# A perceiver layer's first chunk of tokens: order on GpSimd, two banks for its halves, and 48 turns of the identity on TensorE

## What is computed

```python
def reference(x, ctx, w_q, w_kv, w_out, b_out, ...):     # x 32x64x256, ctx 32x1601x192, all float32
    x = x + xattn(layernorm(x), ctx, w_q, w_kv, w_out, b_out)   # 16 heads of 64
    x = x + rwkv(layernorm(x), decay, first, mixes, Wk, Wv, Wr, Wo, bo)
    x = x + relu(layernorm(x) @ w1 + b1) @ w2 + b2
    return x

def xattn(query, context, w_q, w_kv, w_out, b_out):
    q = query @ w_q
    k, v = split(context @ w_kv)
    attn = softmax(q k^T / 8)
    return (attn v) @ w_out + b_out

def layernorm(x):
    return (x - mean(x)) / sqrt(var(x) + 1e-5)
```

## Time and profile before

| | before |
|---|---|
| median of 3 executions | 2353.97 us (2352.03 to 2357.43) |
| the profiled execution, its own time | 2352.82 us |
| its span, first to last instruction | 2351.0 us |
| mean granted TensorE clock | 0.997 |
| busy: PE / DVE / POOL / ACT | 97% / 77% / 70% / 66% |
| start of the first product of `queries(0)` | 18.02 us |
| start of the first product of `with_keys(0)` | 24.58 us |
| start of the first scores of the attention | 134.42 us |

### The profile page before, as it was taken

The page is one execution under the profiler, slowest core; times in us unless marked ns, Lnnn a source line. Parts: engine busy times, 40 slices in busy tenths (PEclk is TensorE's granted clock), DMA queues, the critical chain, the costliest instruction groups (busy, mean ns, idle before and its releaser), DMA issues.

```text
span 2351.0 us, 43942 instructions
## 1 busy us (share of the span) xinstructions
PE 2291.5 (97%) x13696; PEld 2097.1 (89%) x13696; DVE 1812.6 (77%) x3664; ACT 1542.7 (66%) x2696; POOL 1646.7 (70%) x858
## 2 busy tenths in 40 slices
PE   7979999999999999999999999999999999899999
PEld 5769999999999999999999999999999998878788
DVE  7867777777777777777777777777777777679884
ACT  6756666666666666666666666666666666565444
POOL 4238878888888888888888888888888886421111
PEclk9999999999999999999999999999999999999999
DMA  8988888888888888888888888888888886987000
GB/s 228 267 199 189 196 196 197 199 199 200 198 200 199 199 199 199 199 201 199 199 199 199 199 200 199 200 199 200 199 199 199 199 199 162 212 197 198 8 10 28
DMA packets 410273, 438.97 MB, mean 187 GB/s; under 512 B 82528, under 2 KB 380896, under 8 KB 410208
## 3 DMA queue, kind: packets, MB, share of 16 engines
q1 hardware_dynamic: 394384, 427.23, 77.3%
q10 hardware_dynamic: 15824, 10.91, 2.0%
HBM read 167.42 MB, written 52.43 MB: 94 GB/s over the span
## 4 chain that ended last, share of the span: by engine, by line
POOL 44%; issue 25%; PE 18%; SPq 5%; DVE 4%; DMA 2%; ACT 2%; POOLq 0%; ACTq 0%; DVEq 0%
POOL p_pt_lo L640 24%; POOL p_nat L667 7%; POOL p_q_lo L652 5%; POOL p_ct_lo L648 4%; POOL p_ct_hi L659 4%; SPq L441 3%; PE p_scores L1508 3%; PE p_scores L1678 2%; PE p_cols L1665 2%; PE p_scores L1632 2%; PE p_acc L1528 2%; PE p_cols L1574 2%; PE p_scores L1461 1%; DMA p_raw<-o_scratch 1%; PE p_scores L1590 1%
## 5 line engine op out<-in xcount | busy, mean ns | idle before, releaser
L640 POOL TENSOR_TENSOR p_pt_lo<-p_landed,p_pt_hi 128x768 fp32r<-128x768 f32 x504 | 991.1, 1987 | 322.7 <-ACT p_pt_hi L861 322.7
L1528 PE MATMUL p_acc<-p_nat,p_pt_hi 128*128 128x384 f32 x3024 | 887.6, 360 | 7.5 <-POOL p_pt_lo L640 5.7
L1530 PE MATMUL p_acc<-p_nat,p_pt_lo 128*128 128x192 f32 x3024 | 758.2, 251 | 0.0
L897 ACT ACTIVATE p_prob<-p_scores,p_negmax 128x800 f32<-128x800 f32 (+1 forms) x512 | 471.5, 926 | 392.8 <-DVE p_negmax L1222 392.7
L1508 PE MATMUL p_scores<-p_ct_hi,p_q_hi 128*128 128x512 f32 (+2 forms) x2048 | 703.6, 347 | 11.5 <-ACT p_prob L897 11.5
L1508 PE MATMUL p_scores<-p_ct_hi,p_q_lo 128*128 128x512 f32 (+2 forms) x2048 | 703.1, 347 | 0.0
L1528 PEld LDWEIGHTS p_acc<-p_nat,p_pt_hi 128*128 128x128 f32 x3024 | 567.4, 188 | 17.1 <-POOL p_pt_lo L640 10.1
L1530 PEld LDWEIGHTS p_acc<-p_nat,p_pt_lo 128*128 128x128 f32 x3024 | 577.0, 191 | 0.0
L861 ACT ACTIVATE p_pt_hi<-p_landed 128x768 fp32r<-128x768 f32 x504 | 398.6, 838 | 166.0 <-PE p_acc L1532 123.8
L1230 DVE STREAM_TRANSPOSE turned<-p_prob 128x1536 f32<-128x1536 f32 x256 | 452.5, 1768 | 0.0
L1508 PEld LDWEIGHTS p_scores<-p_ct_hi,p_q_hi 128*128 128x128 f32 x2048 | 389.0, 190 | 56.8 <-ACT p_prob L897 12.7
(11 more groups left out here) (229 smaller groups left out, 3126.2 us busy)
## 6 DMA issues: line engine op xcount, KB each, us to landing
p_landed<-turned SPq DMA_DIRECT2D x2032, 104.0 KB, 2.3
resid<-in_ctx SPq DMA_DIRECT2D x128, 288.0 KB, 5.0
o_scratch<-resid SPq DMA_DIRECT2D x256, 96.0 KB, 2.7
qk_scratch<-p_out_a SPq DMA_DIRECT2D x32, 512.0 KB, 5.1
p_stage<-qk_scratch SPq DMA_DIRECT2D x31, 512.0 KB, 3.8
p_stage<-qk_scratch SPq DMA_DIRECT2D x62, 256.0 KB, 4.2
p_stage<-in_ctxT SPq DMA_DIRECT2D x31, 401.0 KB, 4.7
p_stage<-in_ctxT SPq DMA_DIRECT2D x62, 200.5 KB, 5.6
```

Source lines behind the costliest of these rows:

```text
L640: nc.gpsimd.tensor_tensor(pt_lo[:, t0:t1, :, :], by_tile(slot, t0, t1), bits(pt_hi[:, t0:t1, :, :]), ALU.subtract).then_inc(pt_lo_done, 1)
L897: nc.scalar.activation(prob[:, lo:hi], scores[:, S0 + lo:S0 + hi], ACT.Exp, bias=negmax[:, par:par + 1], accum_out=rowsum[:, par, h:h + 1] ...
L1528: nc.tensor.matmul(acc[k % 2][:, 0:2 * DC], pt_hi[:, t, :, :].rearrange("p i x -> p (i x)"), x[:, t, :], start=t == 0, stop=False, skip_gr ...
L1530: nc.tensor.matmul(acc[k % 2][:, 0:DC], pt_lo[:, t, :, :].rearrange("p i x -> p (i x)"), x[:, t, 0:DC], start=False, stop=False, skip_grou ...
```

## The change

Three edits, all at the start of the program, and nothing else in it:

1. On POOL, `query_weights_lo(0)` waits also for `x_normal` >= 4, that is for all four instructions of DVE's `x_normalised(0)`.
2. Half 1 of chunk 0 is turned into another bank (`xp_of(1)` = `qp[2]`, `scores[:, 1536:2048]`) and ACT and DVE read it there; PE's wait for `xp_lo` begins with n = 2 instead of n = 1. All other halves use the bank of before.
3. Ahead of the first turn, PE turns the identity 48 times into `ap[0][:, 0:128]`, which nobody reads, as soon as `x_ident` is made.

```diff
-    SLOTS, QPS = 4, 3
+    SLOTS, QPS, WARM = 4, 3, 48
...
-        xp, qp = scores[:, 0:512], [scores[:, (1 + i) * 512:(2 + i) * 512] for i in range(QPS)]
+        qp = [scores[:, (1 + i) * 512:(2 + i) * 512] for i in range(QPS)]
+        xp_of = lambda n: qp[2] if n == 1 else scores[:, 0:512]
...
             def query_weights_lo(i):
                 half = slice(i * INNER // 2, (i + 1) * INNER // 2)
                 pool.wait_ge(wq_hi_done, i + 1)
+                if i == 0:
+
+                    pool.wait_ge(x_normal, CTT)
                 nc.gpsimd.tensor_tensor(wq_lo[:, :, half], wq[:, :, half], bits(wq_hi[:, :, half]), ALU.subtract).then_inc(wq_lo_done, 1)
...
-                nc.scalar.activation(xT_hi[:, k, c % 2 * CT:(c % 2 + 1) * CT], xp, ACT.Copy).then_inc(xp_hi, 1)
+                nc.scalar.activation(xT_hi[:, k, c % 2 * CT:(c % 2 + 1) * CT], xp_of(n), ACT.Copy).then_inc(xp_hi, 1)
...
-                nc.vector.tensor_tensor(xT_lo[:, k, cols_of], xp, bits(xT_hi[:, k, cols_of]), ALU.subtract).then_inc(xp_lo, 1)
+                nc.vector.tensor_tensor(xT_lo[:, k, cols_of], xp_of(n), bits(xT_hi[:, k, cols_of]), ALU.subtract).then_inc(xp_lo, 1)
...
                 if n == 0:
                     pe.wait_ge(x_ident_done, 2)
-                if n >= 1:
+
+                    for _ in range(WARM):
+                        nc.tensor.transpose(ap[0][:, 0:P], x_ident[:, :], x_ident[:, :])
+                if n >= 2:
                     pe.wait_ge(xp_lo, n)
                 pe.wait_ge(x_normal, (c + 1) * CTT)
                 for t in range(CTT):
-                    last = nc.tensor.transpose(xp[:, t * P:(t + 1) * P], xt[:, c * CTT + t, k * P:(k + 1) * P], x_ident[:, :])
+                    last = nc.tensor.transpose(xp_of(n)[:, t * P:(t + 1) * P], xt[:, c * CTT + t, k * P:(k + 1) * P], x_ident[:, :])
```

## The result

| | before | changed |
|---|---|---|
| median of 15 executions each, side by side | 2355.16 us (2352.03 to 2357.82) | 2360.05 us (2354.95 to 2363.73) |
| ratio of the two, 95% interval | | 1.0019 [1.0012, 1.0026] |
| the profiled execution, own time / span | 2352.82 / 2351.0 us | 2359.53 / 2357.7 us |
| mean granted clock | 0.997 | 0.996 |
| `queries(0)` / `with_keys(0)` / first scores | 18.02 / 24.58 / 134.42 us | 12.16 / 20.43 / 131.37 us |

What follows compares the result with a forecast made beforehand. PE, busy for 97% of the span, was taken to set the pace; of 6.0 us gained by `queries(0)`, the wait for x chunk 1 and the clock left 1.8: 2353.97 - 1.8 = 2352.2 us, range 2348.5 to 2356.5 us.

Steps and rivals of the forecast that it cites:

- What bounds the start: Before `with_keys(0)`: normalisations slowed beside POOL's splits, halves passing one after the other, x chunk 1 landing at 17.0 us.
- Edit 1: Start, DVE: with POOL silent the four normalisations take 1.40 us and end at 9.3 instead of 12.8 us.
- Edit 2: Start, PE: the halves' turns overlap with ACT's and DVE's steps; `queries(0)` starts at 12.0 instead of 18.02 us.
- Edit 3, its size: Start, PE: 48 turns, 0.22 us apart and then 0.11 once the clock rises, end at 8.5 to 9.4 us.
- The rival that the turns don't raise the clock: Start, PE: turns end at 12.0 us, `queries(0)` starts at 15.4; whole kernel 2351.9 us; chance 0.33.
- What is late next, and the clock: After `queries(0)`: x chunk 1's landing holds `with_keys(0)` to 20.6 us, the clock falls in PE's idleness; 1.8 us kept.
- DVE's limit of 2.2: At 28.49 us DVE loses its idle 0.35 us, so its chain can be 2.2 us ahead at most.
- From there on PE hardly waits, and the attention starts 1.8 us earlier: From `with_keys(1)` on: PE waits little, so the 1.8 us lead carries to the attention and the whole time.
- hidden in PE's wait of 12.9 us: Start, PE: lower end of the 48 turns' cost, nothing; the upper end was 10.5 us, to 12.0 us.
- a shift elsewhere: Anywhere, such as another clock fall in the attention's start: 1 to 2 us either way; chance 0.09.
- The rival on the other side: Start, PE: 48 turns into one bank cost 0.45 us each, ending at 23.1 us; 2361 us, slower by 0.3%; chance 0.04.
- The band of 0.2%: Whole kernel: 4.7 us is about what a measurement can tell from no change; chance of staying inside, 0.88.

Runs made afterwards that it cites:

- e12: The kernel before with only the second bank for half 1 of chunk 0, neither the wait on POOL nor the 48 turns: 2353.75 us, ratio 0.9990.
- e2: The kernel before with 94 instructions of already fulfilled semaphore waits on PE before its first turn, none of the three edits: 2361.36 us, ratio 1.0021.
- e3: The kernel before with only the 48 turns of the identity, neither the wait on POOL nor the second bank: 2362.87 us, ratio 1.0024.
- e8: The changed kernel, all three edits, with 81 unread 128x128 products in gaps of the first attention steps: 2353.16 us, ratio 0.9991.

## Why the prediction was wrong

- **What bounds the start**: right. The four normalisations, the two halves in a row, the landing of x chunk 1 at 7.8 + 9.2 us again, and PE's small waits after it.
- **Edit 1**: right in itself, 1.38 us for 1.4, split from 9.50 us for 9.3. e12 shows that it is worth 0.5 us at 43 us and nothing to be seen at the attention's start.
- **Edit 2**: right, `queries(0)` at 12.16 us for 12.0.
- **Edit 3, its size**: right, an end at 9.26 us in 8.5 to 9.4.
- **The rival that the turns don't raise the clock** (0.33) was wrong. At 6.2 us, after 4.6 us of nothing but turns, the turns went from 0.21 to 0.11 us each. The Trainium skill (TensorE: Matmul & The Clock Gate, Part 4: PE-mode transpose) says that turns in transpose mode don't count as busy for the gate; for these turns of 32-bit floats the measurement decides. (The trace lists them as MATMUL and doesn't tell whether they run in the mode that the page means.) That the two cases are worth almost the same is right: with and without turns `with_keys(0)` starts at 20.43 and 20.22 us.
- **What is late next, and the clock**: right, `stack_high(0)` at 19.00 for 19.1, `with_keys(0)` at 20.43 for 20.6, `with_keys(1)` at 25.69 for 25.8 to 26.5. The 2.1 us at 43 us are what DVE's limit of 2.2 allowed.
- **The step that failed** is the one from there to the end: "From there on PE hardly waits, and the attention starts 1.8 us earlier", from which the whole time was to come 1.8 us earlier too. The start of the attention came 3.05 us earlier and was worth nothing at the end, because the sum has no term for the 94 instructions that edit 3 puts ahead of everything on PE's queue, beyond the time that they take themselves. They move all of PE's later instructions by 94 in the blocks in which these are fetched, and with them the moments at which a fetch holds up SyncE's transfers. That costs 0.26% against the quiet places (mean ratio 1.0019 against 0.9993 of the seven kernels at -1, 0, 256 and 257), 6 us; 3.2 of them are seen in the early stretch. The prediction had said "hidden in PE's wait of 12.9 us" for the least of edit 3's cost, and gave 0.09 to "a shift elsewhere", "worth 1 to 2 us either way": the right drawer, but too small and without a mechanism.
- **The rival on the other side** (turns not pipelined, 2361 us) names nearly the measured time by a wrong way: the turns were 0.21 and 0.11 us apart.
- **The band of 0.2%** was called about what a measurement can tell. The control runs bear that out (0.9989 and 1.0000 for the same text), and 0.0019 lies just at its edge; that it isn't scatter rests on the four kernels at 94 and 95, all above 1.001, against seven at -1, 0, 256 and 257, none above 1.0001.
- **The range**: the lower end doesn't follow from its working. Cases from 2351.8 us and times up to 1.9 us under their median give 2349.9 us, not 2348.5. The measured time lies on the other side, so nothing hangs on it.

## What to carry to other kernels

An edit that adds instructions to an engine that never idles is costed in two parts: the time that they take, and what they do to the place of everything behind them. The second can be larger than the gain of the edit and has nothing to do with its idea, so before such an edit is thrown away (or praised) for 0.1 to 0.3%, time it with a few other counts of idle instructions, one of which restores the old place. And a gain of 2 us in the start must be compared with an unchanged control, by medians and by profiles: here the medians' ratio alone wandered by 0.1%, and three profiles of one kernel had spans of 2351.0, 2356.6 and 2358.4 us.

## What was not expected of the hardware

- Where PE's instructions lie modulo 256 changes a kernel of 2355 us by 0.1 to 0.2% (0.3% in one comparison of five runs), in straight code only: nothing was lost in the 1509 us of the loop, in which neither the kernel before nor the changed one fetches an instruction of PE.
- While a block of PE's instructions is fetched, SyncE's issue of a transfer takes up to 2.2 us instead of 0.60 us: 127 issues of over 1 us before the loop, each beside a fetch, none of 29321 in the loop.
- In e2, 94 instructions that wait for a semaphore that is already there take 0.106 us each on PE, and two waits share one.
- Turns of the identity raise the granted clock from its lower level (1.2 GHz) to 2.4 GHz: after 4.6 us of them in the changed kernel and 5.6 us in e3.
- The fall of the clock near 117 us comes or not from one kernel to the next after much the same idle stretch of PE: 2.69 us in the kernel before (low for 3.4 us), 4.06 in e8 (low for 6.8 us), 3.56 in the changed kernel and 2.74 in e12 (no fall). From 43 us to the first scores the lead grows by 1 us in the changed kernel and shrinks by 2 us in e8.
